# Dividing the probabilities on GpSimd before they are transposed, in a Perceiver kernel's first attention

## What is computed

```
q = (layernorm(x) @ W_q), k = context @ W_k, v = context @ W_v     # 8 heads of 64
sim  = q k^T / 8, masked keys to the most negative number
attn = softmax(sim) over the 256 keys of the batch
out  = attn @ v                                                     # per head
x    = x + out @ W_o + b_o
```

## Time and profile before

| what | value |
|---|---|
| median of 3 runs | 1451.44 us (1448.49 to 1451.67) |
| span of the profiled execution | 1580.3 us |
| mean granted clock of PE | 0.948 of full speed |
| phase one in the span | about 0 to 457 us, then its last self-attention until about 475 us |
| PE busy in the span | 1369.1 us (87%) |
| POOL busy in the span | 615.5 us (39%), of it 49 us of phase one (lines 1150, 1244 and 1489) |

### The profile page before, as it was taken

How to read it: one execution, slowest core, us unless ns; L and a number is a source line. 1 busy time by engine, 2 the same in 40 slices (tenths; PEclk the granted TensorE clock), 3 DMA queues, 4 the chain that set the end, 5 groups by cost and what they waited for, 6 DMA issues and landing times. The chain is left out here.

```text
span 1580.3 us, 32555 instructions
## 1 busy us (share of the span) xinstructions
PE 1369.1 (87%) x10653; PEld 1008.8 (64%) x10653; DVE 996.6 (63%) x2910; ACT 618.7 (39%) x1909; POOL 615.5 (39%) x797
## 2 busy tenths in 40 slices
PE   7999999999987989999998998677787887878846
PEld 4666676666754666666666666466676776767645
DVE  3766666666653578867887787546665655544447
ACT  3544545444443566655665565221111111133100
POOL 1101111011101146555655555545556565555630
PEclk9999999999996899999999999889999999998978
DMA  8534244243400011111111111278878777776758
GB/s 257 191 98 142 92 142 138 95 141 100 134 1 28 14 53 53 51 63 63 50 54 64 63 36 40 70 235 266 248 232 245 233 236 250 239 218 204 227 195 351
DMA packets 153404, 221.57 MB, mean 140 GB/s; under 512 B 23789, under 2 KB 111116, under 8 KB 151320
## 3 DMA queue, kind: packets, MB, share of 16 engines
q1 hardware_dynamic: 53912, 97.83, 19.5%
q10 hardware_dynamic: 79456, 86.96, 17.6%
q0 software_dynamic: 19872, 34.71, 6.1%
HBM read 161.16 MB, written 99.61 MB: 165 GB/s over the span
## 5 line engine op out<-in xcount | busy, mean ns | idle before, releaser
L898 POOL DMA_INDIRECT y_d<-y,xg x286 | 278.6, 974 | 200.5 <-DVE y L895 126.7
L890 PE MATMUL bank<-pTC,ex 128*128 128x256 f32 x572 | 193.6, 423 | 73.2 <-ACT ex L884 41.0
L872 DVE COPY ex<-bank 128x256 f32<-128x256 f32 x286 | 120.4, 421 | 173.2 <-PE bank L868 101.9
L884 ACT ACTIVATE ex<-bank 128x128 f32<-128x128 f32 x286 | 77.6, 277 | 381.3 <-PE bank L880 222.0
L880 PEld LDWEIGHTS bank<-ex,pTC 128*128 128x128 f32 x1144 | 184.2, 207 | 51.2 <-issue 34.8
L880 PE MATMUL bank<-ex,pTC 128*128 128x128 f32 x1144 | 190.9, 293 | 17.4 <-issue 16.9
L890 PEld LDWEIGHTS bank<-pTC,ex 128*128 128x128 f32 x572 | 93.2, 205 | 91.0 <-ACT ex L884 48.9
L707 POOL DMA_INDIRECT xs_d<-xw,slot_id x128 | 131.0, 1023 | 34.6 <-issue 30.5
L895 DVE COPY y<-bank 128x256 f32<-128x256 f32 x286 | 120.5, 421 | 30.3 <-PE bank L890 18.1
L406 ACT ACTIVATE ex<-bank,nmC 128x256 f32<-128x256 f32 x256 | 119.5, 488 | 8.6 <-DVE nmC L400 8.1
L868 PE MATMUL bank<-ident,xg 128*128 128x128 f32 x572 | 116.0, 287 | 3.9 <-DMA xg<-xs_d 3.9
(11 more groups left out here) (308 smaller groups left out, 2919.5 us busy)
## 6 DMA issues: line engine op xcount, KB each, us to landing
pTC<-in_wexp SPq DMA_DIRECT2D x286, 256.0 KB
xs_d<-zeros ACTq DMA_DIRECT2D x16, 2448.0 KB, 9.7
xg<-xs_d ACTq DMA_DIRECT2D x143, 272.0 KB
cT<-in_ctx SPq DMA_DIRECT2D x32, 512.0 KB, 3.6
xg<-y_d SPq DMA_DIRECT2D x6, 1024.0 KB, 12.4
y_d<-y,xg POOLq DMA_INDIRECT x286
ex<-y_d SPq DMA_DIRECT2D x3, 1024.0 KB, 15.5
xf_d<-xw SPq DMA_DIRECT2D x16, 128.0 KB, 2.7
```

The lines of the kernel that those rows point to most:

```text
L872: T.done("dve", dve.tensor_copy(xgT[z][:, :, :], bk[:, 0:2 * P].rearrange("p (c n) -> p c n", c=2)))
L884: U.done("act", act.activation(h[z][:, :], bk[:, 0:P], ACT.Silu))
L890: D.done("pe", pe.matmul(bk[:, 0:DIM], h[z][:, :], w[z][:, DIM:2 * DIM], start=True, stop=True))
L898: pool.indirect_dma_start(out=y_d, out_offset=bass.IndirectOffsetOnAxis(ap=who, axis=0), in_=y[:, n, :], in_offset=None, bounds_check=last ...
```

## The change

The exponentials are now divided by their sums while queries are still on the partitions. For each j, DVE takes the reciprocal of two sums (event `r{j}`), POOL multiplies the two 128 by 256 blocks of `sm` in place (event `n{j}`, line 1297 of the new kernel), and only then PE transposes them. The values are now the stationary operand and the transposed probabilities the moving one, so that the product over the keys comes out with the head dimension on the partitions. It is what the output projection needs, so `norm` on DVE and the four transposes of line 1351 are gone, and ACT copies bank 4 itself. Bank 4 is free for the next tile's `xnT` once that copy (`oTe`) is done.

```diff
--- before.py
+++ after.py
@@ -1090,7 +1090,6 @@
         sm = sb("sm", [P, 4, 2, 256])
         nm, sums, rec = sb("nm", [P, H0]), sb("sums", [P, H0]), sb("rec", [P, H0])
         pT = sb("pTA", [P, 4, 2, 2, P])
-        oA = sb("oA", [P, 512])
         oT = sb("oTA", [P, 4, P])
         x1 = pair("x1", [P, DIM])
 
@@ -1245,7 +1244,7 @@
             dve.tensor_scalar(mb[:, :], mk[:, i, :], 1.0, -NEG, ALU.subtract, ALU.mult)
             yield 56.16
             Q.wait(pe, "xn", i)
-            A.wait(pe, "norm", i - 1)
+            A.wait(pe, "oTe", i - 1)
             if i == 0:
                 pe.wait_ge(s_id, 16)
             for c in range(2):
@@ -1281,13 +1280,24 @@
             A.done(i, "dve", last, f"t{j}")
             yield (70.37, 73.86, 75.16, 75.48)[j]
             A.wait(act, f"t{j}", i)
-            A.wait(act, "rec", i - 1)
+            A.wait(act, f"r{j}", i - 1)
             for n in range(2):
                 h = 4 * (j // 2) + 2 * n + j % 2
                 last = act.activation(sm[:, j, n, :], sm[:, j, n, :], ACT.Exp, bias=nm[:, h:h + 1], scale=-1.0, accum_out=sums[:, h:h + 1])
             A.done(i, "act", last, f"e{j}")
-            yield (71.64, 68.09, 76.48, 78.62)[j]
-            A.wait(pe, f"e{j}", i)
+            yield (70.90, 73.90, 75.40, 76.20)[j]
+            A.wait(dve, f"e{j}", i)
+            A.wait(dve, f"n{j}", i - 1)
+            mine = slice(4 * (j // 2) + j % 2, 4 * (j // 2) + j % 2 + 3, 2)
+            A.done(i, "dve", dve.reciprocal(rec[:, mine], sums[:, mine]), f"r{j}")
+            yield (70.90, 73.90, 75.40, 76.20)[j]
+            A.wait(pool, f"r{j}", i)
+            for n in range(2):
+                h = 4 * (j // 2) + 2 * n + j % 2
+                last = pool.tensor_scalar(sm[:, j, n, :], sm[:, j, n, :], rec[:, h:h + 1], None, ALU.mult)
+            A.done(i, "pool", last, f"n{j}")
+            yield (71.64, 74.20, 76.48, 78.62)[j]
+            A.wait(pe, f"n{j}", i)
             if j == 0:
                 Q.wait(pe, "qT", i)
             elif j == 1:
@@ -1324,36 +1334,22 @@
         def gather(i):
             z = i % 2
             yield 89.20
-            A.wait(dve, ("e0", "e1", "e2", "e3"), i)
-            A.done(i, "dve", dve.reciprocal(rec[:, :], sums[:, :]), "rec")
-            yield 89.20
             for j in range(2, 4):
                 A.wait(pe, f"pT{j}e", i)
             for q in range(4):
                 K.wait(pe, f"v{q}e", i)
-            for h in range(H0):
-                j, n = 2 * (h // 4) + h % 2, h // 2 % 2
-                for c in range(2):
-                    for b in range(2):
-                        last = pe.matmul(bank[4][64 * b:64 * b + 64, D0 * h:D0 * h + D0], pT[:, j, n, c, 64 * b:64 * b + 64],
-                                         vv[z][:, 2 * b + c, D0 * h:D0 * h + D0], start=(c == 0), stop=(c == 1))
+            for m in range(4):
+                for b in range(2):
+                    for c in range(2):
+                        for f in range(2):
+                            h, j, n = 2 * m + f, 2 * (m // 2) + f, m % 2
+                            last = pe.matmul(bank[4][64 * f:64 * f + 64, m * P + 64 * b:m * P + 64 * b + 64], vv[z][:, 2 * b + c, D0 * h:D0 * h + D0],
+                                             pT[:, j, n, c, 64 * b:64 * b + 64], start=(c == 0), stop=(c == 1))
             A.done(i, "pe", last, "pv")
-            yield 90.79
-            A.wait(dve, "pv", i)
-            A.wait(dve, "rec", i)
-            A.wait(dve, "oT", i - 1)
-            A.done(i, "dve", dve.tensor_tensor(oA[:, :].rearrange("p (h d) -> p h d", h=H0), bank[4][:, :].rearrange("p (h d) -> p h d", h=H0),
-                                               bc(rec[:, :].rearrange("p (h o) -> p h o", o=1), 2, D0), ALU.mult), "norm")
-            yield 90.09
-            A.wait(pe, "norm", i)
-            A.wait(pe, "pT3e", i)
-            for m in range(4):
-                last = pe.transpose(bank[5][:, m * P:(m + 1) * P], oA[:, m * P:(m + 1) * P], ident[:, :])
-            A.done(i, "pe", last, "oT")
             yield 90.65
-            A.wait(act, "oT", i)
+            A.wait(act, "pv", i)
             A.wait(act, "yp", i - 1)
-            A.done(i, "act", act.copy(oT[:, :, :], bank[5][:, :].rearrange("p (m n) -> p m n", m=4)), "oTe")
+            A.done(i, "act", act.copy(oT[:, :, :], bank[4][:, :].rearrange("p (m n) -> p m n", m=4)), "oTe")
             yield 93.81
             if i == 0:
                 fetched(pe, "o")
```

## The result

| | before | after |
|---|---|---|
| median of 4 runs, us | 1451.31 | 1527.38 (1521.89 to 1531.68) |
| ratio, with its 95% interval | | 1.0528 (1.0502 to 1.0554) |
| span of the profiled execution, us | 1580.3 | 1520.6 |
| phase one, to the first keys of phase two, us | 457.99 | 537.88 |
| most frequent periods of a tile, us | 28.19 | 32.23 and 33.92 |

The account below looks back on a forecast made before the run. PE was taken to bound phase one; three new waits of 1.22, 1.27 and 0.61 us make 3.10 us a tile, over 15 tiles 46.5 us on 1451.44, so 1498 us, range 1465 to 1524 us.

Parts of the forecast that it names:

- What bounds the kernel: Phase one: PE is busy 34.98 of 35 us, so every microsecond that PE waits is a microsecond of the kernel.
- The hand-over and the reciprocals: Before POOL's multiplications: 0.19 us for a reciprocal on DVE and 0.05 us for each hand-over between engines.
- POOL's duration T: One POOL multiplication of a 128 by 256 block: 0.73 us, and 0.09 more for the first of a burst.
- The first wait: PE before the transposes of j = 0, waiting for POOL: 1.22 us per tile.
- the second: PE before the transposes of j = 2 and 3, waiting for POOL: 1.27 us more per tile.
- the third: PE before the next tile's `xnT`, waiting for ACT's copy: 1.05 us, less 0.44 for removed transposes, 0.61 net.
- The clock, costed at nothing: PE's granted clock in phase one: stays at 1.00 despite the waits, with PE busy for 89%.
- The first and the last tile: Ends of phase one: each gives only a part, so the loss is counted for 15 of 16 tiles.
- The rest lets the delay through: Behind phase one: nothing depends on the change, so the whole delay of 46.5 us reaches the kernel's time.
- POOL's time grows in proportion: Rival on POOL's multiplications: T = 1.01 us in proportion to line 626, 5.05 us a tile, 1527 us; chance 0.11.
- POOL multiplies at the rate of its copies: Rival on POOL's multiplications: T = 0.41 us, 1.2 us a tile, 1469 us; chance 0.18.
- PE's full share hides slack: Rival on PE in phase one: the waits lie in hidden gaps, only removed transposes count, 1445 us; chance 0.07.

Follow-up runs that it names:

- two tensors: The changed kernel with POOL multiplying the block by the reciprocals repeated along it, instead of by a scalar column: +34 us over the kernel before, one run.
- the retimed kernel: The changed kernel with the product in bank 5 and PE's transposes moved behind other work: -2 us against the kernel before, ratio 0.9966 to 1.0001.

## Why the prediction was wrong

Its direction and its three waits were right, at the places named and with the releasers named; its size was not, 47 us against 76. By its own steps:

- **What bounds the kernel.** Right. PE was full, and every wait that was made or removed showed in the period.
- **The hand-over and the reciprocals.** Right: `r0` begins at 317.70, ends at 317.86, and POOL begins 0.10 us behind its end. The reciprocal took 0.16 us where I had 0.19, and the hand-overs 0.10 us here and 0.14 from ACT to PE (338.19 to 338.33) where I had 0.05 or none.
- **POOL's duration T, 0.73 us.** This step failed. It measured 0.92 (0.91 from start to start in a burst). I had taken the two-tensor time of the same width, because line 626 without the 0.09 us of a first instruction was as long as a two-tensor product of 160 columns. Taking off the 0.09 was the error: the 128 multiplications take 920 to 933 ns and those by a constant 845 to 859 ns, first or not. As it stood, line 626 was 1.19 times the two-tensor product (629 against 529 ns), and 1.19 times 729 is 867 ns, near the 848 that the constant took. The column of scalars adds 75. The bound above, line 626 in proportion to the columns (1.01), was nearer than the value taken. At the forecast's slope, (0.92 - 0.73) x 6 us = 1.1 us a tile less the 2 x 0.09 of the first instructions; measured, the clean period is 32.23 against 31.3 us, 0.94 x 14 = 13 us.
- **The first wait**, 1.22 forecast, 1.44 measured; **the second**, 1.27 and 1.82; **the third**, 0.61 net and 0.67.
- **The clock, costed at nothing.** This step failed as well. I had looked at a stretch in which PE was 91% busy at 1.00. The share of phase one became 88%, and the granted clock fell for a part of 8 of 14 periods, 1.69 us each: 13.5 us. A mean over 35 us said nothing about waits of 1.1 to 1.4 us that lie close together.
- **The first and the last tile**, counted together as 3.1 us. Tile 0 lost 6.1 us (its successor's `xnT` comes at 37.73 instead of 31.67) and the last tile 3.7 (from its `xnT` to the first keys of phase two 35.04 us instead of 31.38). In tile 0 nothing of a self-attention stands between the transposes:

```profile
24.41 0.66 PE L1310 MATMUL bank<-ident,sm 128*128 128x128 f32 x4 [2.48 <-POOL sm L1297]
26.21 1.05 PE L1310 MATMUL bank<-ident,sm 128*128 128x128 f32 x4 [1.14 <-POOL sm L1297]
```

Some of it is clock, 0.57 on average from 26 to 30 us: the second row takes 1.05 us for what takes 0.66 above. These tiles and the two steps above make 14 x 0.94 + 8 x 1.69 + 6.7 = 33.4 us, the whole difference between the 79.9 us of phase one and the 46.5 forecast.
- **The rest lets the delay through.** Nearly: 79.9 us at the first keys of phase two, 74.6 at the third (608.54 against 533.98), 76 in the runs.
- **The rivals.** "POOL's time grows in proportion" had the right total, 1527, by half the right reason: T was 0.92 and not 1.01, and the clock made up for it. That it met the time is luck. "POOL multiplies at the rate of its copies" is refuted, and for this multiplication so is the rule of the Trainium skill, GPSIMD Engine Reference, section Engine selection, that one input goes at roughly line rate: here one input took 0.85 to 0.92 us and two inputs 0.61. "PE's full share hides slack" is refuted: the waits of 3.93 us made the period 4.04 us longer, so none of them was hidden.

## What to carry to other kernels

When an engine is full and executes in order, a step put on an idle engine costs only as far as the full engine waits for its end (here 6 us a tile for each us of a multiplication, and none once the order was changed): work out when the full engine arrives and when the event comes, and move the consumer behind other work in the same edit. Count each repeated wait twice, once for itself and once for the clock that it may cost. A bank is a thing to wait for as well, and its release can come onto the full engine's path: here the choice of another PSUM bank for the product was worth some 16 us of the 76 (+60 against +76, from two sets).

## What the runs showed of the hardware

- On GpSimd, multiplying 128 by 256 float32 in place takes 923 ns with a column of scalars, 848 ns with a constant, and 613 ns as a product of two tensors whose second one is repeated along the columns. I had not expected the form with more inputs to be the fastest.
- TensorE's granted clock fell to its lower level in 8 and, in a second trace, in 9 of 14 periods when it waited about 1.4, 1.8 and 1.1 us in a tile of 32 us. Without the 1.1 us it fell in 5 of 14; with one wait of 1.1 us a tile, with waits of 0.4 and 1.0 us, or of 0.6, 0.3 and 1.0 us (two tensors), in none. Transposes of the identity in the waits, with 0.4 and 0.3 us of them left, kept it at 1.00.
- A burst of four 128 by 512 matmuls takes 1.72 us from its start to the next between two full-width bursts, 1.81 or 1.82 us with matmuls of 64 or 32 rows on one side, and 1.91 us with them on both (the retimed kernel's rows). The order of bursts on a full engine has a price of its own, 0.24 us a tile here.
